# Delta rule: keys used unnormalised with one factor per token, level sums through a standing identity, keys turned by VectorE blocks and a bounce through DRAM

## The reference

```
q, k, v = split(silu(causal_conv(hidden @ w_qkv)));  q = l2norm(q);  k = l2norm(k)
per value head, token by token, with the state St (128 x 128):
    St    = St * exp(g_t)
    delta = (v_t - k_t @ St) * beta_t
    St    = St + outer(k_t, delta)
    o_t   = (q_t / sqrt(128)) @ St
out = (rmsnorm(o) * silu(hidden @ w_z)) @ w_out
```

## Time and profile before

| what | value |
|---|---|
| three timed runs | 3311.48, 3311.82, 3314.59 us; median 3311.82 us |
| span of the profiled execution | 3310.8 us (its page gives no other time for it) |
| TensorE busy | 3215.4 us, 97% of the span |
| VectorE, GpSimd, ScalarE busy | 2448.0 (74%), 1859.5 (56%), 1550.6 us (47%) |
| mean granted TensorE clock | 0.992 of full speed |

### The profile page before, as it was taken

The page is one execution under the profiler, slowest core; times in us unless marked ns, Lnnn a source line. Parts: engine busy times, 40 slices in busy tenths (PEclk is TensorE's granted clock), DMA queues, the critical chain, the costliest instruction groups (busy, mean ns, idle before and its releaser), DMA issues. The chain is left out here.

```text
span 3310.8 us, 60236 instructions
## 1 busy us (share of the span) xinstructions
PE 3215.4 (97%) x20576; PEld 2131.6 (64%) x20576; DVE 2448.0 (74%) x3686; ACT 1550.6 (47%) x4983; POOL 1859.5 (56%) x1824
## 2 busy tenths in 40 slices
PE   5899999999999999999999999999979999999999
PEld 2577777777777777777777777777754444454444
DVE  6899999999999999999999999999940011034453
ACT  2465656565656565556555655565531000022232
POOL 2677777777777777777777777777730000011132
PEclk8999999999999999999999999999999999999999
DMA  2133333323333233323333332333325222211001
GB/s 94 48 77 84 77 72 74 85 70 74 80 84 75 69 80 76 77 70 83 80 75 73 80 81 70 77 79 81 81 62 207 76 102 102 76 39 64 0 13 39
DMA packets 423119, 248.75 MB, mean 75 GB/s; under 512 B 306688, under 2 KB 372352, under 8 KB 417280
## 3 DMA queue, kind: packets, MB, share of 16 engines
q1 hardware_dynamic: 421520, 237.81, 27.5%
q10 hardware_dynamic: 1296, 7.08, 0.5%
HBM read 156.39 MB, written 71.57 MB: 69 GB/s over the span
## 5 line engine op out<-in xcount | busy, mean ns | idle before, releaser
L736 PE MATMUL acc<-xT,wc 128*128 128x512 f32 x2048 | 934.8, 599 | 2.7 <-PEq L112 2.0
L736 PEld LDWEIGHTS acc<-xT,wc 128*128 128x128 f32 x2048 | 369.7, 190 | 372.6 <-issue 372.0
L1015 DVE SCALAR_TENSOR_TENSOR d_conv<-acc,wc,d_conv 128x511 f32<-128x511 f32 (+2 forms) x768 | 566.8, 738 | 41.8 <-ACT d_conv L1190 32.6
L749 PE MATMUL acc<-wc,xT 128*128 128x256 f32 x2048 | 473.4, 384 | 0.0
L749 PEld LDWEIGHTS acc<-wc,xT 128*128 128x128 f32 x2048 | 379.1, 190 | 46.2
L1541 PE MATMUL acc<-t_area 128*128 128x512 f32 x768 | 332.5, 592 | 1.6 <-ACT t_area L1990 1.6
L634 POOL TENSOR_TENSOR d_bf<-d_kks,d_gam 128x512 f32<-128x512 f32 x128 | 160.6, 1277 | 294.9 <-ACT d_kks L1234 294.9
L2047 POOL TENSOR_SCALAR t_veps<-t_mv 128x1 f32<-128x1 f32 x32 | 9.7, 303 | 547.0 <-DVE t_mv L1786 547.0
L1048 DVE STREAM_TRANSPOSE d_em<-d_dm 128x1024 f16<-128x1024 f16 x256 | 314.5, 1228 | 2.2
L1776 DVE TENSOR_TENSOR t_x<-acc,t_x 128x512 f32<-128x512 f32 x16 | 11.1, 691 | 392.3 <-PE acc L1541 392.3
L1055 DVE TENSOR_TENSOR d_zm<-d_tz,cons 128x512 f16<-128x512 f32 x384 | 259.0, 674 | 52.0 <-PE d_tz L799 47.0
(11 more groups left out here) (228 smaller groups left out, 7002.3 us busy)
## 6 DMA issues: line engine op xcount, KB each, us to landing
d_decay<-decay_rows SPq DMA_DIRECT2D x64, 512.0 KB, 5.2
v_rows<-d_vb SPq DMA_DIRECT2D x256, 128.0 KB, 2.3
d_vn<-v_rows SPq DMA_DIRECT2D x64, 512.0 KB, 3.7
core_rows<-d_ob SPq DMA_DIRECT2D x1024, 32.0 KB, 1.7
t_area<-core_rows SPq DMA_DIRECT2D x30, 1024.0 KB, 4.8
wc<-in_w SPq DMA_DIRECT2D x96, 256.0 KB, 3.2
d_qn<-d_qf SPq DMA_DIRECT2D x1024, 16.0 KB, 1.8
t_x<-in_x SPq DMA_DIRECT2D x4, 1024.0 KB, 9.2
```

What stands on the lines that cost most here:

```text
L736: last = nc.tensor.matmul(bank(TILE[j])[:, :], wtile(j, k), xT[:, k, r % B * S:(r % B + 1) * S], start=k == 0, stop=k == KT - 1)
L749: last = nc.tensor.matmul(bank(f"z{j}")[:, i * GV * P:(i + 1) * GV * P].rearrange("p (h n) -> p h n", h=GV), xT[:, k, r % B * S + (2 * j + ...
L1015: nc.vector.scalar_tensor_tensor(c[:, d:S], bank(TILE[j])[:, 0:S - d], tap(j, KS - 1 - d), c[:, d:S], ALU.mult, ALU.add).then_inc(taps, 1)
```

## The change

- Keys stay raw. `kT` is the direct output of `silu(n, 0)`, and `k_turn`, `normal_k`, `khat_turn` and `copy_kT` are gone with their eight TensorE transposes per item. Keys with tokens on partitions are made by a VectorE transpose of 32 x 32 blocks (`flip_k`) and a bounce through DRAM (`store_k`: four DMAs; `load_k`: one, behind them on SP).
- The factor per token goes into what is made from keys: `copy_kk` and `copy_kq` become four ScalarE copies each, one per chunk, with a scale; the values are multiplied by the inverse factor (`scale_v`, four ScalarE copies, new); the end decay gets it too. `k_norm` has three GpSimd instructions instead of two and stands behind `o_gate`.
- `zm` starts as the identity instead of zeros, and the mask step writes only the blocks of its level (`copy_predicated` in place of a multiplication). The product of `level_d` and `level_e` then contains the old blocks already, and the VectorE additions (four d, two e per item) become ScalarE copies: `copy_d` at all six levels with one instruction each, `copy_e` at levels 4 and 5.
- The signs move: B is held negated, and `refine` adds.

The core of the diff:

```diff
+            def store_k(n):
+                sp.wait_ge(k_flipped, count(n))
+                wait(sp, k_moved, at(back(n, 1), 80, 80))
+                for a in range(NC):
+                    sp.dma_start(k_dram[n[1] % 2].rearrange("b i a n -> a i b n")[a],
+                                 kf[a * 32:(a + 1) * 32].rearrange("p b c j -> p b (c j)")).then_inc(k_moved, 16)
+            def load_k(n):
+                sp.wait_ge(k_moved, at(n, 80, 64))
+                wait(sp, ks_ready, at(back(n, 2), GV, GV))
+                sp.dma_start(kn[n[1] % 2][:, :, :, :].rearrange("p a c j -> p (a c j)"), ...).then_inc(k_moved, 16)
...
             def k_norm(n):
-                nc.gpsimd.tensor_tensor(rk[:, :], rkt[:, :], cons[:, C_POW:C_POW + NC], ALU.pow).then_inc(rk_ready, 1)
+                nc.gpsimd.tensor_tensor(rk[n[1] % 2][:, :, :], bc(rkt[:, :], 2), cons[...], ALU.pow).then_inc(rk_ready, 1)
+                pool.wait_ge(rk_ready, at(n, 3, 2))
+                nc.gpsimd.tensor_tensor(bend, bend, bc(rk[n[1] % 2][:, 0, :], GV), ALU.mult).then_inc(rk_ready, 1)
...
-            def k_turn(n):
-                turn(bank("k_turn"), kraw, k_turned)
-            def khat_turn(n):
-                turn(bank("khat_turn"), khat[n[1] % 2], khat_turned)
             def kk(n):
-                pe.wait_ge(kT_ready, count(n))
+                pe.wait_ge(silued, nth(n, "silued", 0))
...
             def level_z(m, l):                                  # TensorE
-                elif l < 5:
-                    pe.wait_ge(d_added, at(m, 4, l))
                 else:
-                    pe.wait_ge(d_copied, at(m, 3, 2))
+                    pe.wait_ge(d_copied, at(m, LEVELS, l))
...
             for l in range(LEVELS):                             # VectorE
-                nc.vector.memset(zm[l][:, :], 0.0).then_inc(zeros_set, 1)
+                nc.vector.tensor_copy(zm[l][:, :]..., bc(cons[:, C_ID:C_ID + P], GV * NC)).then_inc(zm_set, 1)
+            def flip_k(n):
+                dve.wait_ge(silued, nth(n, "silued", 0))
+                nc.vector.transpose(kf[:, :, :, :], kT[third(n)]...).then_inc(k_flipped, 1)
             def level_z(m, l):
-                nc.vector.tensor_tensor(even(zm[l], l), packed(tz, l), bc(mask, GV * NC), ALU.mult).then_inc(z_ready, 1)
-            def level_d(m, l):
-                nc.vector.tensor_tensor(even(dm, l), packed(td, l), even(dm, l), ALU.add).then_inc(d_added, 1)
-            def level_e(m, l):
-                nc.vector.tensor_tensor(odd(e, l), packed(te, l), odd(e, l), ALU.add).then_inc(e_added, 1)
+                nc.vector.copy_predicated(even(zm[l], l), bc(mask, GV * NC), packed(tz, l)).then_inc(z_ready, 1)
...
             def copy_kk(n):                                     # ScalarE; copy_kq alike
-                nc.scalar.activation(kks[:, :], bank("kk")[:, :], ACT.Copy).then_inc(kk_copied, 1)
+                for c in range(NC):
+                    nc.scalar.activation(chunk(kks, c), chunk(bank("kk"), c), ACT.Copy, scale=rk[n[1] % 2][:, 0, c:c + 1]).then_inc(kk_copied, 1)
+            def scale_v(s):
+                act.wait_ge(v_moved, at(s, 80, 80))
+                for c in range(NC):
+                    nc.scalar.activation(v, v, ACT.Copy, scale=rk[s[1] % 2][:, 1, c:c + 1]).then_inc(v_scaled, 1)
+            def copy_d(m, l):
+                act.wait_ge(d_done, at(m, LEVELS, l + 1))
+                nc.scalar.activation(even(dm, l), packed(td, l), ACT.Copy).then_inc(d_copied, 1)
+            def copy_e(m, l):
+                nc.scalar.activation(odd(em[m[1] % 2], l), packed(te, l), ACT.Copy).then_inc(e_copied, 1)
             def slot(n, project, invert, recur, finish):        # ScalarE
-                    copy_d(s, 5, 0)
+                    scale_v(s)
+                    copy_d(s, 5)
+                    copy_e(s, 5)
...
+                    copy_d(m, 0)          # ahead of solved(s, 0)
...
                     first_state(s)
+                if invert:
+                    copy_d(m, 1)
                 if finish:
                     o_scale(f, 0)
                     o_scale(f, 1)
+                    k_square(n)
                     copy_kq(m)
                     first_output(s)
+                    copy_d(m, 2)
...
                     copy_kk(n)
+                    copy_d(m, 3)
```

More of the change, by code:

```diff
@@ L10 @@
 BF16 = mybir.dt.bfloat16
+I32 = mybir.dt.int32
 ALU = mybir.AluOpType
@@ L709, in slot @@
                 if project:
+                    k_norm(n)
                     gate_strict(n, 0)
@@ L752, in z_tile @@
                 last.then_inc(z_projected, 1)
-            def turn(dst, src, sem_):
-                for c in range(NC):
-                    last = nc.tensor.transpose(chunk(dst, c), chunk(src, c), cons[:, C_ID:C_ID + P])
-                last.then_inc(sem_, 1)
             def products(dst, left, right, sem_):
@@ L1035, in flip_q @@
                 nc.vector.transpose(qf[:, :, :, :], qT[third(m)][:, :].rearrange("p (c b j) -> p b c j", c=NC, b=NC)).then_inc(v_flipped, 1)
+            def flip_k(n):
+                dve.wait_ge(silued, nth(n, "silued", 0))
+                wait(dve, k_moved, at(back(n, 1), 80, 64))
+                nc.vector.transpose(kf[:, :, :, :], kT[third(n)][:, :].rearrange("p (c b j) -> p b c j", c=NC, b=NC)).then_inc(k_flipped, 1)
             def flip_o(s):
@@ L1125, in slot @@
                     refine(s, 1)
+                if project:
+                    flip_k(n)
                 if invert:
@@ L1194, in silu @@
                 if j == 0:
-                    wait(act, k_turned, count(n, 1))
+                    wait(act, ks_s, at(back(n, 3), 3, 3))
                 if j >= 2:
@@ L1211, in k_square @@
             def k_square(n):
-                act.wait_ge(k_turned, count(n))
-                wait(act, rk_ready, at(back(n, 1), 2, 1))
+                act.wait_ge(k_moved, at(n, 80, 80))
+                wait(act, rk_ready, at(back(n, 1), 3, 1))
                 wait(act, k_squares, at(back(n, 1), NC, NC))
-                squares(lambda c: chunk(bank("k_turn"), c), lambda c: junk[:, c, :], kss, k_squares)
+                squares(lambda c: kn[n[1] % 2][:, :, c, :], lambda c: junk[:, c, :].rearrange("p (a j) -> p a j", j=32), kss, k_squares)
             def q_square(n):
@@ L1240, in o_scale @@
                     nc.scalar.activation(o, o, ACT.Copy, scale=r2[:, h, c:c + 1]).then_inc(o_scaled, 1)
-            def normal_k(n):
-                act.wait_ge(k_turned, count(n))
-                act.wait_ge(rk_ready, at(n, 2, 2))
-                wait(act, ks_ready, at(back(n, 2), GV, GV))
-                for c in range(NC):
-                    nc.scalar.activation(chunk(khat[n[1] % 2], c), chunk(bank("k_turn"), c), ACT.Copy, scale=rk[:, c:c + 1]).then_inc(khat_ready, 1)
             def copy_kq(m):
```

138 lines of the change are left out of this document (64 added, 74 removed).

## The result

| what | before | after |
|---|---|---|
| median of the timed runs | 3312.2 us (3311.5 to 3314.6, four) | 3382.6 us (3382.2 to 3383.1, four) |
| span of the profiled execution | 3310.8 us | 3380.9 us |
| TensorE busy | 3215.4 us, 97% | 3202.4 us, 95% |
| VectorE, ScalarE busy | 74%, 47% | 66%, 53% |

The ratio is 1.021 (95% interval 1.0195 to 1.0224): 70 us slower. The forecast was 3378.

A forecast was written before the change was run, and what follows sets the result against it. TensorE, busy 498.88 of 500 us, sets the pace. Per full slot -0.28 + 0.57 + 0.66 = +0.95 us, times 61 is +58; weight slots +3, start +5: +66, so 3378 us, slower, own range 3350 to 3405.

The forecast's parts named there:

- TensorE's removed work: `k_turn` and `khat_turn`, 0.47 us each: 0.94 us per slot, 57 us over 61 slots if nothing else came late.
- B: `level_d(m, 1)` to `solve(s, 1)`: 6.09 becomes 6.66 us, +0.57, as `copy_d(m, 1)` delays the chain from `o_scale` to the residual.
- C: `solve(s, 1)` to the next `level_z(s, 4)`: 3.83 becomes 4.49 us, +0.66, with `copy_d(m, 3)` behind `copy_kk` on ScalarE.
- rival 1: TensorE stays packed, both ScalarE copies come in time and the whole 0.94 us is kept: 3263 us; chance 0.08.
- rival 2: Only one chain binds, at `solve(s, 1)` (3338 us) or at `level_z(s, 4)` (3315 us, no change); chance 0.10.
- A: `close(s, 0)` to `solve(s, 0)`: 1.87 becomes 1.59 us, a gain of 0.28, since `solve` waits for VectorE's last `close`.
- The rest of the slot: VectorE's relief returns nothing, `copy_predicated` costs 0, longer `k_norm` and DRAM bounce are hidden; `scale_v` costs 3 us in weight slots.
- rival 3: `copy_predicated` in VectorE's mask step is slow: 3436 us at 1.2 us each, 3560 at 1.9; chance 0.10.
- rival 4: Keys come late from DRAM, each us beyond the slack adding 61 us between `level_d(m, 1)` and `solve(s, 1)`; chance 0.02.
- The weight slots: 15 slots with new weights: `scale_v` ahead of `copy_d` makes `refine` wait, 0.2 us each, +3 us, bounds 0 and 15.
- The start: First slot only: first `copy_kk` waits for flip, both transfers, squares and norm; TensorE idle, +5 us, bounds 0 and 7.
- The signs: Profile marks: slot about 37.5 us, idle 0.6 or more before `solve(s, 1)` and `level_z(s, 4)`, VectorE down 5 points, ScalarE up 12.

The follow-up runs named there:

- `kk` in the hole: Changed kernel with the eight `kk` matmuls moved on TensorE from behind `grow(s, 1)` to ahead of `solve(s, 1)`: 3354.0 us, 1.0123 of before.
- three calls: Kernel with level 1 and 3 copies on VectorE, plus `attend(s, 1)` ahead of `read_k(s, 2)` and three `z_tile(s, 0)` calls around `solve(s, 0)`: 3319.3 us, 1.002.
- one gained 16: Kernel with level 1 and 3 copies on VectorE, plus `attend(s, 1)` ahead of `read_k(s, 2)` and one `z_tile(s, 0)` call ahead of `solve(s, 0)`: 3291.5 us, 0.993.

## Why the prediction was right

- **TensorE's removed work, and B and C.** Right in mechanism and size: +0.53 and +0.69 for +0.57 and +0.66. The two waits rule out rival 1. Taking the level 1 copy out of ScalarE's queue takes B's wait away; the level 3 copy, C's. The two nearly add, as the prediction said against rival 2: alone 52.5 and 20.5 us, together 67.6.
- **A.** -0.33 for -0.28. But the step stopped at the start of `solve(s, 0)`. Its two followers are slower too, +0.22 in the next stretch, so A gained only 0.11. That was left out: the turn had also covered ScalarE's scaled queries, for which `attend(f, 3)` waits. This is why a slot takes 37.64 and not 37.47. The experiment with the turns put back says the same of the removed work: it was worth about 9 us, little more than A's 0.11 in 61 slots.
- **The rest of the slot.** `copy_predicated` at 691 ns: the nearest row was the right one, and rival 3 is out. The DRAM bounce is hidden, since `k_square` runs right behind `o_scale`: rival 4 is out. The weight slots had the wrong sign, -5.6 for +3: probably since C's wait now gives the late first tap its time in each slot. The kernels without that wait fit this, with 0.75 above a normal slot for level 3 on VectorE and some 0.95 for `kk` in the hole, but nothing else was tried.
- **The start.** +7.2 for +5, just beyond the bounds of 0 to 7. The bounce was priced for the first slot, and there TensorE waits for the first `copy_kk` (its timeline, before and after):

```profile
87.99 7.60 PE L736 MATMUL acc<-xT,wc 128*128 128x512 f32 x17 [0.78 <-ACT d_kks L1234]
```
```profile
89.25 6.21 PE L762 MATMUL acc<-xT,wc 128*128 128x512 f32 x9 [7.41 <-ACT d_kks L1230]
```

  From the first projection to here it is 21.69 us, 17.95 before: 3.7 of the 7.2. The rest lies in the next two slots, in which not all four items are in flight; the prediction has no term for them, so it is in part luck that +5 came near.
- **The rule against sums off VectorE** (the Trainium skill, page "ScalarE: Activation LUTs", section "Rules for kernel authors"): its factor is for bf16, and for these f32 to f16 copies out of PSUM there is no sign of it. The copies take 0.60 us on ScalarE; on VectorE, in the kernel with both moved, 0.68 to 0.69.
- **The transposes.** The 390 ns that the prediction takes from the Trainium skill (page "TensorE: Matmul & The Clock Gate", section "Part 4: PE-mode transpose") are for bf16; those here are f32. The sum does not use it.
- **The signs.** Two came short: the wait ahead of `level_z(s, 4)` is 0.53 us, where 0.6 or more was named, and ScalarE's share rose by 8 points in the window of the earlier trace rows, where about 12 was named.

The total, +70 for +66, came so near because the misses cancel: the slot was 0.17 too short (10.6 us in 61), the weight slots gave back 8.6 of that, the start added 2.2, and the earlier first projection and what follows the slots (-2.5 and +2.4), of which the prediction says nothing, cancel each other.

## What to carry to other kernels

Work that leaves the busiest engine is worth its time only where nothing else lasts that long beside it; put the same work back, unread, and see what it costs (here 9 of 57 us). An instruction that is moved to a less busy engine is priced by what stands behind it in that queue, not by its length: two copies of 0.6 us cost 68 us, four others gave 35. When a hole is filled with work from elsewhere, look at which chain starts behind that work: against the same kernel without it, three calls lost 12 us and one gained 16. And when a wait goes, ask whose result comes late next: here it was that of GpSimd, which had stood idle for a quarter of the time in the changed kernel.

## What the runs showed that was not expected

- TensorE counts as busy through many short waits. In the kernel with both copies on VectorE it is busy 496.77 of 500 us and still loses 0.75 of 36.33 us a slot; only the distances between starts, and the weight loads, show it.
- Behind a product that waited, the next f32 product starts later than it otherwise does, 0.54 to 0.55 us behind `solve(s, 1)` for 0.45, though what follows there (`read_q(s, 1)`, the state times the queries) needs none of its results. Which part of that is its weight load, which then starts late, was not told apart.
- GpSimd's lengths moved both ways though its instructions did not change: means between 500 and 2300 us of 1283 ns before and 1733 after for `p_full`, 1166 and 1508 for the masking of `em`, 1636 and 1157 for `i_minus_d`. The long ones lie beside VectorE's scan (L1024 before, L1028 after): in the changed kernel the masking of `em` takes 1.15 to 1.18 us where no scan runs beside it, and 2.07 (median) where one does, though a few beside a scan are short too. Why was not tried. It matters where VectorE waits for GpSimd, as at A above.
